# Attention on one core of a Trainium2: features of two heads at a time, and other products ahead of attention's

## The chip, the core and the metric

One core of a Trainium2 chip runs the whole program in one launch. The metric is the time of one execution on the device in microseconds (us); the median of the runs counts. TensorE (PE) multiplies, VectorE (DVE) and ScalarE (ACT) read its results from PSUM (8 banks of 128 partitions x 512 float32), GpSimd (POOL) gathers rows, SyncE (SP) starts transfers.

## The reference

1250 rows of 512 features pass a graph network of three layers, a mixture of 16 experts, a second graph network with linear attention, and a last layer with a choice of 128 of 1024 values. The change is in the third stage, and in a small part of the second:

```python
q, k, v = (heads(h_dense, Wq), heads(h_dense, Wk), heads(h_dense, Wv))   # 256 rows, 8 heads of 64
u = jnp.einsum('bhnd,md->bhnm', t * scale, proj)                         # features, m = 256, for q and for k
kf, qf = jnp.exp(u - diag - max) / np.sqrt(M) + KEPS                     # max: over m for q, over all for k
kv = jnp.einsum('bhnm,bhnd->bhmd', kf, vm)
z = 1.0 / (jnp.einsum('bhnm,bhm->bhn', qf, kf.sum(axis=2)) + KEPS)
attn = jnp.einsum('bhnm,bhmd->bhnd', qf, kv) * z[..., None]
conv_out = jax.nn.relu((A @ xn / deg) @ W_conv + b_conv)                 # A: counts of edges, 1250 x 1250
```

The experts compute `silu(x @ gate) * (x @ up) @ down` for the rows that chose them.

## The kernel before, in words

Every engine has a program written out by hand; semaphores alone tie them together. Rows are kept in 10 tiles of 125. There is no planner: the order of each engine's program is the order of the work, and each engine takes its instructions in that order.

*Preparation of attention* (`tensor`, `vector`). TensorE makes the key features of the 8 heads (`pe_features`, L1987; head h lies on partitions 64 to 127 of its operands where h is odd, on 0 to 63 where it is even) into three banks in turn, VectorE takes their maximum (L1706), and the bank is used again when it has. After heads 2 and 5 a product of z (`pe_conv_z`: one tile of normalised rows times W_conv, L444) is put between. Then the maxima are turned (L2223), z 2 follows, the bias of the keys is spread by a small product (L2226), z 3 follows. Each z is split by ScalarE (`act_z_hi`, L767) and VectorE (`vec_z`, L1103) into a high and a low part.

*The loop over heads.* In turn t (0 to 8) TensorE does `pe_head_products` of head t-1, `pe_head_features` of head t, and `conv_work[t]`: two products of z in turns 0 to 2, one sum over the neighbours in turns 3 to 8 (`pe_conv_sum`, `pe_neighbours`, L1850; 20 products of 125 x 512). `pe_head_products` is: values' product (kf with v, bank 4, L2002), turning of the query features (bank 5, L2010), a wait for ScalarE's copy of them (L879) and VectorE's copy of kv (L1291), attention's product (bank 4 again, L2017). ScalarE takes the exponentials of the features (L866, L872), VectorE scales them (L1276, L1284), finds the query's maximum and bias between (L1278, L1281), and normalises attention's result (L1294 to L1299). ScalarE also copies the edge counts of tile t-2 in turn t (`act_counts`, L778). Banks 0 to 3 hold the features: 0 and 1 for even heads, 2 and 3 for odd ones. After the loop the attention rows are turned (L2244) and the last sums follow.

*The experts' steps* (`pe_step`, 8 executed here). Two experts' rests of 32 rows each are worked on together: gate and up products on strips of 32 columns (L1906), ScalarE's silu (L811), VectorE's product (L1241), turning of the hidden rows (L1915) for each of the two, with the turning of the next rows (L1872) between, VectorE's copies (L1244), down products on strips of 32 columns (L1922). Both hidden parts are turned before the first down product.

## Time and profile before

| | us |
|---|---|
| median of 3 runs | 1354.39 |
| lowest, highest | 1353.56, 1357.17 |
| the profiled execution | 1357.98 |
| its span, first to last instruction | 1356.3 |

| engine | busy us | share of the span |
|---|---|---|
| TensorE, products | 1270.0 | 94% |
| TensorE, loading of weights (beside them) | 835.9 | 62% |
| VectorE | 557.9 | 41% |
| ScalarE | 462.7 | 34% |
| GpSimd | 199.3 | 15% |

The times of the program's span are counted from its first instruction. A product of float32 operands shows as two instructions. A busy TensorE is not TensorE at its peak: it is also busy at half clock, and with few rows or columns. The mean granted clock of the span was 0.98 of 2.4 GHz.

### The profile page before, as it was taken

The numbers are of one execution on the slowest core, as the hardware profiler recorded it, in microseconds if no ns is written. First come the engines' busy times: TensorE is split into PE (matmuls) and PEld (weight loads), VectorE is DVE, ScalarE is ACT, GpSimd is POOL, SyncE is SP. The second block draws the span as 40 slices with busy tenths as digits, with TensorE's granted clock in tenths as the row PEclk, the third lists the DMA queues.
The fourth block names the chain that finished last, engine by engine and source line by source line (L and its number), as shares of the span: only waits on it lengthen the run. The fifth ranks groups of instructions, "written<-read, shape, count | busy, mean of one in ns | idle before, by whom it ended". The sixth has DMA issues, their size and how long they took to land.

```text
span 1356.3 us, 19368 instructions
## 1 busy us (share of the span) xinstructions
PE 1270.0 (94%) x6567; PEld 835.9 (62%) x6568; DVE 557.9 (41%) x1512; ACT 462.7 (34%) x991; POOL 199.3 (15%) x201
## 2 busy tenths in 40 slices
PE   4899999999999999989999999999999999989697
PEld 2454477466556645468877887777465576564465
DVE  8999832211124425100000000001483333686894
ACT  5799643122212210011111111111132232337893
POOL 2000000000000006511111111111543000022480
PEclk8999999999999999999999999999998999999899
DMA  9100000000021120571165213456460000100001
GB/s 220 75 1 1 2 1 1 1 1 1 0 94 31 32 94 2 162 272 58 43 232 200 83 46 137 152 214 221 126 190 19 32 1 1 71 1 0 1 28 50
DMA packets 42949, 98.25 MB, mean 72 GB/s; under 512 B 4113, under 2 KB 6603, under 8 KB 41845
## 3 DMA queue, kind: packets, MB, share of 16 engines
q1 hardware_dynamic: 28613, 68.70, 14.9%
q0 software_dynamic: 6144, 16.45, 4.3%
q10 hardware_dynamic: 8112, 12.08, 2.4%
q8 instruction: 45, 0.74, 0.2%
q14 instruction: 35, 0.29, 0.1%
HBM read 81.02 MB, written 16.17 MB: 72 GB/s over the span
## 4 chain that ended last, share of the span: by engine, by line
PE 72%; DVE 13%; issue 4%; POOL 4%; ACT 3%; DMA 2%; ACTq 1%; DVEq 1%; POOLq 0%
PE psum L444 34%; PE psum L1850 14%; PE psum L1893 7%; PE psum L1830 4%; PE psum L2044 3%; POOL slot_tokens L705 3%; PE psum L1987 2%; DVE sb_hT_conv L1447 1%; PE psum L1922 1%; PE psum L472 1%; ACT sb_htok L828 1%; DVE sb_stats L452 1%; PE psum L1872 1%; POOL sb_blk L649 1%; DVE sb_htok L1336 1%
## 5 line engine op out<-in xcount | busy, mean ns | idle before, releaser
L444 PEld LDWEIGHTS psum<-sb_blk,sb_w_reg 128*128 128x128 f32 x1792 | 204.0, 192 | 14.3 <-issue 14.3
L444 PE MATMUL psum<-sb_blk,sb_w_reg 128*128 128x128 f32 x1792 | 205.2, 275 | 3.2 <-issue 3.2
L1850 PE MATMUL psum<-sb_z_reg_r,sb_hT_conv_r 125*125 125x512 f32 x400 | 169.6, 424 | 0.2 <-issue 0.2
L444 PE MATMUL psum<-sb_w_reg,sb_hT_conv 128*125 128x512 f32 (+1 forms) x376 | 168.9, 599 | 0.0
L1233 DVE TENSOR_TENSOR sb_blk<-sb_blk,psum 128x256 f32<-128x256 f32 x56 | 23.6, 421 | 285.5 <-ACT sb_blk L799 285.5
L1850 PE MATMUL psum<-sb_htok_r,sb_hT_conv_r 125*125 125x512 f32 x300 | 117.8, 393 | 0.0
L444 PEld LDWEIGHTS psum<-sb_w_reg,sb_hT_conv 128*125 128x125 f32 (+1 forms) x376 | 69.0, 189 | 77.5 <-issue 76.9
L444 PE MATMUL psum<-sb_hT_conv,sb_w_reg 128*128 128x416 f32 (+3 forms) x336 | 102.1, 460 | 0.8 <-issue 0.8
L1893 PE MATMUL psum<-sb_w_reg,sb_blk 128*128 128x512 f32 x224 | 100.8, 592 | 0.0
L778 ACT CAST sb_hT_conv_r<-sb_a_reg 125x625 fp32r<-125x625 f32 x80 | 56.1, 715 | 115.0 <-PE psum L1850 115.0
L1850 PEld LDWEIGHTS psum<-sb_z_reg_r,sb_hT_conv_r 125*125 125x125 f32 x400 | 75.1, 188 | 25.1 <-issue 7.7
L2044 PE MATMUL psum<-sb_hT_conv,sb_sil 125*125 125x400 bf16 x316 | 73.1, 356 | 16.0 <-DVE sb_a_reg L1455 7.0
L2044 PEld LDWEIGHTS psum<-sb_hT_conv,sb_sil 125*125 125x125 bf16 x316 | 42.5, 139 | 69.9 <-DVE sb_a_reg L1455 38.3
L444 PEld LDWEIGHTS psum<-sb_hT_conv,sb_w_reg 128*128 128x128 f32 x336 | 63.6, 193 | 34.6 <-issue 31.2
L1830 PE MATMUL psum<-sb_w_reg,sb_hT_conv 128*125 128x512 f32 x160 | 80.4, 593 | 0.8 <-DMA sb_w_reg<-w_gnn 0.8
L1447 DVE TENSOR_SCALAR sb_hT_conv<-sb_sil,sb_blk 125x400 bf16<-125x400 f16 x316 | 81.1, 327 | 0.0
L799 ACT ACTIVATE sb_blk<-psum 128x256 f32<-128x256 f32 x56 | 21.5, 383 | 172.0 <-PE psum L444 172.0
L891 ACT ACTIVATE sb_blk<-sb_sil,sb_blk 125x125 bf16<-125x125 f16 x237 | 77.3, 391 | 7.1 <-DVE sb_blk L1409 5.6
L691 POOL IOTA sb_blk<- 125x160 f32 x1 | 0.3, 307 | 462.2 <-DVE sb_blk L1130 462.2
L1850 PEld LDWEIGHTS psum<-sb_htok_r,sb_hT_conv_r 125*125 125x125 f32 x300 | 55.7, 186 | 17.2 <-issue 4.8
L1893 PEld LDWEIGHTS psum<-sb_w_reg,sb_blk 128*128 128x128 f32 x224 | 40.4, 190 | 40.2 <-issue 40.2
L767 ACT CAST sb_z_reg_r<-psum 125x512 fp32r<-125x512 f32 x40 | 23.3, 583 | 91.8 <-PE psum L444 86.0
(396 smaller groups left out, 1774.8 us busy)
## 6 DMA issues: line engine op xcount, KB each, us to landing
sb_hT_conv<-w_expert SPq DMA_DIRECT2D x7, 2048.0 KB, 8.9
sb_w_reg<-w_expert SPq DMA_DIRECT2D x6, 2048.0 KB, 17.6
sb_hT_conv<-w_expert SPq DMA_DIRECT2D x7, 1024.0 KB
slot_outs<-sb_blk ACTq DMA_DIRECT2D x28, 256.0 KB
sb_w_reg<-w_expert SPq DMA_DIRECT2D x6, 1024.0 KB, 19.4
sb_w_reg<-w_gnn SPq DMA_DIRECT2D x1, 4096.0 KB, 42.6
sb_w_reg<-w_qkv SPq DMA_DIRECT2D x1, 3072.0 KB, 21.6
slot_outs<-sb_blk ACTq DMA_DIRECT2D x1, 2560.0 KB, 10.8
```

Source lines behind the costliest of these rows:

```text
L444: ins = e.matmul(out, l, r, start=(n == 0), stop=(n == len(pairs) - 1))
L705: e.indirect_dma_start(list_dram, bass.IndirectOffsetOnAxis(ap=list_i[:, i, k:k + 1], axis=0), tok_id[:, i:i + 1], None).then_inc(list_sca ...
L767: e.copy(z_hi_rows[i], psum[0:TP, b, :]).then_inc(z_hi, 1)
L778: e.copy(counts_at(l, n), adj[:, h * HALF_T:(h + 1) * HALF_T, tile(i)]).then_inc(counts_in, 1)
L891: e.activation(sq_lo[t % 2][:, j, :], neg_iota, ACT.Square, bias=neg_lo[:, c:c + 1], scale=-1.0).then_inc(lo_squared, 1)
L1233: e.tensor_tensor(hidT[:, 2 * h:2 * h + 2, :].rearrange("p k n -> p (k n)"), silg[:, h, :], psum[:, 1 + h, HF:2 * HF], ALU.mult).then_inc( ...
L1447: e.tensor_scalar(hot_key[n][:, j, :], key_iota, key[:, c:c + 1], None, ALU.is_equal).then_inc(hot_ready, 1)
L1830: ins = e.matmul(psum[0:TP, bank, :], hT[:, k, tile(i)], w_gnn[:, 0 if own else 1, k, :], start=(k == 0), stop=(k == KD - 1))
L1850: ins = e.matmul(psum[0:TP, b, :], counts_at(l, 2 * i + n // NT)[:, s % HALF_T, :], z[s], start=(n == 0), stop=(n == len(pairs) - 1))
L1893: ins = e.matmul(psum[:, 5, :], hidT[:, k, :], w_dn[:, k, :], start=(k == 0), stop=(k == KD - 1))
L1987: ins = e.matmul(psum[:, b, s * 256:(s + 1) * 256], qk[n][rows, h // 2, s * 128:(s + 1) * 128], projT[rows, :], start=True, stop=True)
L2044: ins = e.matmul(psum[0:TP, t % 3, 0:KEYS], hot_lo[n][:, j, :], hot_key[n][:, j, :], start=(j == 0), stop=(j == RUN - 1))
```

## The change

Five things, all in the order and the grouping of instructions; what is computed stays the same.

- Features are made for a pair of heads: the even head's and the odd head's products alternate (rows 0 to 63, rows 64 to 127), each into its own bank, keys first, then queries. In the loop this is done in every second turn. Their semaphore is `features_mm`.
- In the preparation the four pairs follow each other over banks 1 to 4; the products of z come after them, and the small products use banks 5 and 4.
- `pe_head_products` becomes `pe_head_values` (values' product, turning) and `pe_head_attention`. Between the two stand, in even turns, the next pair's features, and in odd turns the first piece of the turn's other work: one z, or half a sum. `pe_neighbours` can be issued in halves.
- VectorE copies kv, then does the next head's features (maximum and bias before the scaling of the keys), then attention's part. Values' product of head h waits for attention's part of head h-1.
- In `pe_step` the second hidden part is turned behind the first down product. The second load of the shared down weights counts on the first one's semaphore.

```diff
@@ -407,9 +407,15 @@
         XN_COEF = KD + 1
         DIAG_MM, KM_MM, KMAX_TURNED, K_BIAS_MM = 1, 9, 10, 11
         MEAN_W, HALF, V_ONES, DIAG, KM_READ, K_MAX8, K_DIAG, K_BIAS = 1, 4, 5, 6, 14, 15, 17, 19
-        head_pe, head_vec, head_act = (sem("head_" + n) for n in ("pe", "vec", "act"))
-        K_MM, Q_MM, KV_MM, QF_TURNED, ATT_MM, PER_HEAD_PE = 1, 2, 3, 4, 5, 5
-        KF, Q_BIAS, QF, KV_IN, ATT, PER_HEAD_VEC = 1, 2, 3, 4, 6, 6
+        head_pe, head_vec, head_act, features_mm = (sem("head_" + n) for n in ("pe", "vec", "act", "features"))
+        KV_MM, QF_TURNED, ATT_MM, PER_HEAD_PE = 1, 2, 3, 3
+        K_MM, Q_MM, PER_PAIR_PE = 2, 4, 4
+        PER_HEAD_VEC = 6
+
+        def vec_at(first, later):
+            return lambda h: first if h == 0 else PER_HEAD_VEC * h + later
+        Q_BIAS_AT, KF_AT, QF_AT = vec_at(1, -1), vec_at(2, 0), vec_at(3, 1)
+        KV_IN_AT, ATT_AT = vec_at(4, 4), vec_at(9, 9)
         KF_EXP, QF_EXP, QFT_IN, PER_HEAD_ACT = 2, 4, 5, 5
         at_turned, attnT_in, ha_mm, ha_in, shifted = (
             sem(n) for n in ("at_turned", "attnT_in", "ha_mm", "ha_in", "shifted"))
...
@@ -1272,23 +1278,25 @@
 
         def vec_head_features(e, h):
             r, bq = h % 2, 2 * (h % 2) + 1
+            e.wait_ge(features_mm, PER_PAIR_PE * (h // 2) + Q_MM)
+            e.tensor_reduce(q_max[:, :, h], psum[:, bq, :].rearrange("p (t m) -> p t m", t=2), AX.X,
+                            ALU.max).then_inc(v_own, v.up())
+            e.wait_ge(v_own, v.n)
+            e.scalar_tensor_tensor(q_bias[:, :, h], diag[:, 0, :, h], -1.0, q_max[:, :, h], ALU.mult,
+                                   ALU.subtract).then_inc(head_vec, 1)
             e.wait_ge(head_act, PER_HEAD_ACT * h + KF_EXP)
             e.tensor_scalar(kf[:, r], kf[:, r], inv_root_m, K_EPS, ALU.mult, ALU.add).then_inc(head_vec, 1)
-            e.wait_ge(head_pe, PER_HEAD_PE * h + Q_MM)
-            e.tensor_reduce(q_max[:, :, h], psum[:, bq, :].rearrange("p (t m) -> p t m", t=2), AX.X,
-                            ALU.max).then_inc(v_own, v.up())
-            e.wait_ge(v_own, v.n)
-            e.scalar_tensor_tensor(q_bias[:, :, h], diag[:, 0, :, h], -1.0, q_max[:, :, h], ALU.mult,
-                                   ALU.subtract).then_inc(head_vec, 1)
             e.wait_ge(head_act, PER_HEAD_ACT * h + QF_EXP)
             e.tensor_scalar(qf[:, r], qf[:, r], inv_root_m, K_EPS, ALU.mult, ALU.add).then_inc(head_vec, 1)
 
-        def vec_head_products(e, h):
+        def vec_head_values(e, h):
             r = h % 2
             e.wait_ge(head_pe, PER_HEAD_PE * h + KV_MM)
             if h >= 2:
                 e.wait_ge(head_pe, PER_HEAD_PE * (h - 2) + ATT_MM)
             e.tensor_copy(kv[:, r].rearrange("p m d -> p (m d)"), psum[:, 4, 0:130]).then_inc(head_vec, 1)
+
+        def vec_head_attention(e, h):
             out = psum[:, 4, 0:130].rearrange("p (t d) -> p t d", t=2)
             e.wait_ge(head_pe, PER_HEAD_PE * h + ATT_MM)
...
@@ -1702,28 +1710,30 @@
                 e.tensor_scalar(hT[:, k, :], hT[:, k, :], bsc[:, k:k + 1], bsh[:, k:k + 1], ALU.mult,
                                 ALU.add).then_inc(xn_ready, 1)
             for h in range(HEADS):
-                e.wait_ge(prep_pe, DIAG_MM + h + 1)
-                e.reduce_max(k_max[:, h:h + 1], psum[:, 1 + h % 3, :], AX.X).then_inc(prep_vec, 1)
-                if h % 3 == 2:
-                    vec_z(e, 3, h // 3, 6 + h // 3 % 2, conv_lo_rows)
+                e.wait_ge(prep_pe, DIAG_MM + h // 2 * 2 + 2)
+                e.reduce_max(k_max[:, h:h + 1], psum[:, 1 + h % 4, :], AX.X).then_inc(prep_vec, 1)
+            vec_z(e, 3, 0, 6, conv_lo_rows)
             e.wait_ge(prep_pe, KMAX_TURNED)
-            e.reduce_max(k_max8, psum[0:HEADS, 4, 0:128], AX.X).then_inc(prep_vec, 1)
+            e.reduce_max(k_max8, psum[0:HEADS, 5, 0:128], AX.X).then_inc(prep_vec, 1)
             e.wait_ge(prep_vec, K_MAX8)
             e.tensor_scalar(k_diag, ident[0:HEADS, 0:HEADS], k_max8, None, ALU.mult).then_inc(prep_vec, 1)
             e.memset(ones8, 1.0).then_inc(prep_vec, 1)
-            vec_z(e, 3, 2, 6, conv_lo_rows)
+            vec_z(e, 3, 1, 7, conv_lo_rows)
             e.wait_ge(prep_pe, K_BIAS_MM)
             for s in range(2):
-                e.scalar_tensor_tensor(k_bias[:, s, :], diag[:, 1, s, :], -1.0, psum[:, 5, 0:HEADS], ALU.mult,
+                e.scalar_tensor_tensor(k_bias[:, s, :], diag[:, 1, s, :], -1.0, psum[:, 4, 0:HEADS], ALU.mult,
                                        ALU.subtract).then_inc(prep_vec, 1)
-            vec_z(e, 3, 3, 7, conv_lo_rows)
+            for i in range(2, Z_BEFORE):
+                vec_z(e, 3, i, 6 + i % 2, conv_lo_rows)
             e.wait_ge(ld_norms, 3 * 16)
 
             for t in range(HEADS + 1):
                 for h in of_tiles(t, 1, 0, HEADS):
-                    vec_head_products(e, h)
+                    vec_head_values(e, h)
                 for h in of_tiles(t, 0, 0, HEADS):
                     vec_head_features(e, h)
+                for h in of_tiles(t, 1, 0, HEADS):
+                    vec_head_attention(e, h)
                 for what, i in conv_work[t]:
                     if what == "z":
...
@@ -1832,26 +1842,31 @@
             if k == KD - 1:
                 ins.then_inc(self_mm if own else z_mm, 1)
 
-        def pe_neighbours(e, flag, l, i, b, lo_rows):
+        def pe_neighbours(e, flag, l, i, b, lo_rows, halves=(0, 1)):
 
             pairs = [(s, z) for s in range(NT) for z in (z_hi_rows, lo_rows)]
+            steps = range(halves[0] * NT, (halves[-1] + 1) * NT)
             with e.If(flag > 0):
-                for n, (s, z) in enumerate(pairs):
+                for n in steps:
+                    s, z = pairs[n]
                     if n % NT == 0:
                         e.wait_ge(counts_in, 2 * (l * NT + i) + n // NT + 1)
                     ins = e.matmul(psum[0:TP, b, :], adj[:, s, tile(i)], z[s].bitcast(F32), start=(n == 0), stop=(n == len(pairs) - 1))
...
@@ -1910,12 +1925,11 @@
             e.wait_ge(ld_down[LAST_SLOT], landing)
             e.wait_ge(s_y, g + 1)
             e.wait_ge(s_he, g * 2 + 2)
-            for n in range(2):
+            for n, (_, w_dn) in enumerate((b, a_)):
                 e.wait_ge(s_hid, g * 2 + n + 3)
                 e.transpose(psum[:, 3 + n, 0:128], hid[:, n * 128:(n + 1) * 128], ident).then_inc(s_ht, 1)
                 if n == 0:
                     pe_turn_rows(e, g + 1)
-            for n, (_, w_dn) in enumerate((b, a_)):
                 e.wait_ge(s_he, g * 2 + n + 3)
                 for k in range(KD):
                     for c in range(PER_BLOCK):
...
@@ -1949,11 +1963,17 @@
                 e.wait_ge(z_lo, 3 * NT + i - 1)
             pe_z(e, 3, i, w_conv, 6 + i % 2)
 
-        def pe_conv_sum(e, flag, i):
+        def pe_conv_sum(e, flag, i, halves=(0, 1)):
             e.wait_ge(z_lo, 4 * NT)
             if i >= 2:
                 e.wait_ge(conv_added, i - 1)
-            pe_neighbours(e, flag, 3, i, 6 + i % 2, conv_lo_rows)
+            pe_neighbours(e, flag, 3, i, 6 + i % 2, conv_lo_rows, halves)
+
+        def pe_conv_work(e, flag, what, i, half):
+            if what == "z":
+                pe_conv_z(e, i)
+            else:
+                pe_conv_sum(e, flag, i, (half,))
 
         def pe_busy(e, b, operand, n, rows=128):
...
@@ -1981,28 +2001,31 @@
             if c % 2 == 1 or c == IN_PAIRS - 1:
                 ins.then_inc(ia_mm, 1)
 
-        def pe_features(e, n, h, b):
-            rows = slice(64 * (h % 2), 64 * (h % 2) + 64)
+        def pe_features(e, n, p, banks, done):
+
             for s in range(2):
-                ins = e.matmul(psum[:, b, s * 256:(s + 1) * 256], qk[n][rows, h // 2, s * 128:(s + 1) * 128],
-                               projT[rows, :], start=True, stop=True)
-            return ins
-
-        def pe_head_features(e, h):
-            if h >= 2:
-                e.wait_ge(head_act, PER_HEAD_ACT * (h - 2) + QF_EXP)
-            pe_features(e, 1, h, 2 * (h % 2)).then_inc(head_pe, 1)
-            pe_features(e, 0, h, 2 * (h % 2) + 1).then_inc(head_pe, 1)
-
-        def pe_head_products(e, h):
+                for odd in range(2):
+                    rows = slice(64 * odd, 64 * odd + 64)
+                    ins = e.matmul(psum[:, banks[odd], s * 256:(s + 1) * 256], qk[n][rows, p, s * 128:(s + 1) * 128],
+                                   projT[rows, :], start=True, stop=True)
+                    if s == 1:
+                        ins.then_inc(done, 1)
+
+        def pe_pair_features(e, p):
+            if p >= 1:
+                e.wait_ge(head_act, PER_HEAD_ACT * (2 * p - 1) + QF_EXP)
+            pe_features(e, 1, p, (0, 2), features_mm)
+            pe_features(e, 0, p, (1, 3), features_mm)
+
+        def pe_head_values(e, h):
             r = h % 2
-            e.wait_ge(head_vec, PER_HEAD_VEC * h + KF)
+            e.wait_ge(head_vec, KF_AT(h) if h == 0 else ATT_AT(h - 1))
             for m in range(2):
                 for s in range(2):
                     ins = e.matmul(psum[:, 4, m * 65:(m + 1) * 65], kf[:, r, s, m * 128:(m + 1) * 128],
                                    v_ext[:, s, h, :], start=(s == 0), stop=(s == 1))
             ins.then_inc(head_pe, 1)
-            e.wait_ge(head_vec, PER_HEAD_VEC * h + QF)
+            e.wait_ge(head_vec, QF_AT(h))
             if h >= 1:
                 e.wait_ge(head_act, PER_HEAD_ACT * (h - 1) + QFT_IN)
...
@@ -2010,8 +2033,11 @@
                     ins = e.transpose(psum[:, 5, m * 256 + s * 128:m * 256 + (s + 1) * 128],
                                       qf[:, r, s, m * 128:(m + 1) * 128], ident)
             ins.then_inc(head_pe, 1)
+
+        def pe_head_attention(e, h):
+            r = h % 2
             e.wait_ge(head_act, PER_HEAD_ACT * h + QFT_IN)
-            e.wait_ge(head_vec, PER_HEAD_VEC * h + KV_IN)
+            e.wait_ge(head_vec, KV_IN_AT(h))
             for s in range(2):
                 for m in range(2):
...
@@ -2213,31 +2239,34 @@
             ins.then_inc(prep_pe, 1)
             e.wait_ge(ld_proj, 4 * 16)
             e.wait_ge(ld_wconv, 16)
-            for h in range(HEADS):
-                if h >= 3:
-                    e.wait_ge(prep_vec, DIAG + h - 2)
-                pe_features(e, 1, h, 1 + h % 3).then_inc(prep_pe, 1)
-                if h % 3 == 2:
-                    pe_conv_z(e, h // 3)
+            for p in range(HEADS // 2):
+                if p >= 2:
+                    e.wait_ge(prep_vec, DIAG + 2 * p - 2)
+                pe_features(e, 1, p, (1 + 2 * (p % 2), 2 + 2 * (p % 2)), prep_pe)
+            pe_conv_z(e, 0)
             e.wait_ge(prep_vec, KM_READ)
-            e.transpose(psum[0:HEADS, 4, 0:128], k_max, ident).then_inc(prep_pe, 1)
-            pe_conv_z(e, 2)
+            e.transpose(psum[0:HEADS, 5, 0:128], k_max, ident).then_inc(prep_pe, 1)
+            pe_conv_z(e, 1)
             e.wait_ge(prep_vec, K_DIAG)
-            e.matmul(psum[:, 5, 0:HEADS], ones8, k_diag, start=True, stop=True).then_inc(prep_pe, 1)
-            pe_conv_z(e, 3)
+            e.matmul(psum[:, 4, 0:HEADS], ones8, k_diag, start=True, stop=True).then_inc(prep_pe, 1)
+            for i in range(2, Z_BEFORE):
+                pe_conv_z(e, i)
 
             e.wait_ge(prep_vec, K_BIAS)
             e.wait_ge(hT_in, 5 * NT)
             for t in range(HEADS + 1):
+                beside = [("z", i, None) if what == "z" else (what, i, half) for what, i in conv_work[t]
+                          for half in ((None,) if what == "z" else (0, 1))]
                 for h in of_tiles(t, 1, 0, HEADS):
-                    pe_head_products(e, h)
-                for h in of_tiles(t, 0, 0, HEADS):
-                    pe_head_features(e, h)
-                for what, i in conv_work[t]:
-                    if what == "z":
-                        pe_conv_z(e, i)
-                    else:
-                        pe_conv_sum(e, flag, i)
+                    pe_head_values(e, h)
+                if t % 2 == 0 and t < HEADS:
+                    pe_pair_features(e, t // 2)
+                else:
+                    pe_conv_work(e, flag, *beside.pop(0))
+                for h in of_tiles(t, 1, 0, HEADS):
+                    pe_head_attention(e, h)
+                for work in beside:
+                    pe_conv_work(e, flag, *work)
             e.wait_ge(head_vec, PER_HEAD_VEC * HEADS)
             for s in range(2):
                 for k in range(KD):
```

Left out: the same halves in the other branch of `pe_neighbours`, ScalarE's waits (for `features_mm` and `Q_BIAS_AT(h)`), and the renamed semaphore.

## Rows read from the trace of the kernel before

**Rows 1.** The page, part 4: shares of the chain that ended last, by engine.

```profile
PE 72%; DVE 13%; issue 4%; POOL 4%; ACT 3%; DMA 2%; ACTq 1%; DVEq 1%; POOLq 0%
```

**Rows 2.** Chain of waits in order of time: start us, us, engine, what, line.

```profile
1045.81 7.06 PE psum L444 x16
...
1078.71 0.60 ACT sb_w_reg L879
...
1080.46 3.71 PE psum L1987 x8
1084.17 6.25 PE psum L1850 x20
1090.42 0.84 PE psum L2002 x8
1091.26 0.46 PE psum L2010 x4
...
1091.74 0.59 ACT sb_w_reg L879
...
1092.38 1.11 PE psum L2017 x8
1093.48 1.92 PE psum L1987 x8
1095.41 4.84 PE psum L1850 x20
...
1139.07 0.88 PE psum L2244 x8
```

**Rows 3.** Stretches: length, busy of each engine, PEclk, DMA share, GB/s.

```profile
1019.00:1025.60 6.60, 6.56 (x17) 3.80 (x17) 4.34 (x10) 2.75 (x2) 2.06 (x2) 0.50 0.19 73
...
1080.60:1087.10 6.50, 6.50 (x15) 4.68 (x16) 2.42 (x8) 2.81 (x6) 0.00 (x0) 0.50 0.07 26
1114.70:1118.00 3.30, 3.30 (x8) 2.15 (x8) 1.71 (x4) 1.90 (x6) 0.00 (x0) 0.51 0.00 0
```

**Rows 4.** Timeline of PE, whole and cut at 0.25 us (first, last two).

```profile
1043.82 0.48 PE L1987 MATMUL psum<-sb_blk,sb_w_reg 64*128 64x256 f32 x1
...
1027.96 0.49 PE L1987 MATMUL psum<-sb_blk,sb_w_reg 64*128 64x256 f32 x2
...
1019.15 3.77 PE L1987 MATMUL psum<-sb_blk,sb_w_reg 64*128 64x256 f32 x12
...
1027.96 1.99 PE L1987 MATMUL psum<-sb_blk,sb_w_reg 64*128 64x256 f32 x12
...
1036.18 0.27 PE L2223 MATMUL psum<-sb_ident,sb_blk 128*8 128x128 f32 x1 [1.53 <-DVE sb_blk L1706]
```

**Rows 5.** Timeline of DVE, preparation and one turn of the loop.

```profile
1020.17 1.77 DVE L1702 TENSOR_SCALAR sb_hT_conv<-sb_hT_conv,sb_blk 128x1250 f32<-128x1250 f32 x2
1021.86 1.88 DVE L1706 TENSOR_REDUCE sb_blk<-psum 128x1 f32<-128x512 f32 x3
...
1093.92 0.47 DVE L1299 TENSOR_SCALAR sb_blk<-psum,sb_blk 128x64 f32<-128x64 f32 x2
...
1097.58 0.43 DVE L1284 TENSOR_SCALAR sb_w_reg<-sb_w_reg 128x512 f32<-128x512 f32 x1 [0.91 <-ACT sb_w_reg L872]
```

**Rows 6.** Timeline of all engines: one of the experts' steps.

```profile
683.70 0.33 PE L1915 MATMUL psum<-sb_ident,sb_blk 128*128 128x128 f32 x1
...
683.86 0.60 PE L1872 MATMUL psum<-sb_ident,sb_blk 128*128 128x128 f32 x4
684.07 0.29 DVE L1244 COPY sb_blk<-psum 128x128 f32<-128x128 f32 x1 [0.42 <-PE psum L1915]
...
684.61 0.33 PE L1915 MATMUL psum<-sb_ident,sb_blk 128*128 128x128 f32 x1
...
684.86 1.08 PE L1922 MATMUL psum<-sb_hT_conv,sb_blk 128*32 128x128 f32 x32
...
687.00 0.44 PE L1922 MATMUL psum<-sb_w_reg,sb_blk 128*32 128x128 f32 x5 [0.20 <-issue]
```

More of the change, by code:

```diff
@@ L354, in build @@
         ld_edges, ld_x, ld_w0, ld_w1, ld_router = (sem("ld_" + n) for n in ("edges", "x", "w0", "w1", "router"))
-        ld_shared_up, ld_shared_down, ld_kept = (sem("ld_shared_" + n) for n in ("up", "down", "down_again"))
+        ld_shared_up, ld_shared_down = (sem("ld_shared_" + n) for n in ("up", "down"))
         ld_up = [sem(f"ld_slot{n}_up") for n in range(3)]
@@ L860, in act_head_features @@
             r, bk, bq = h % 2, 2 * (h % 2), 2 * (h % 2) + 1
-            e.wait_ge(head_pe, PER_HEAD_PE * h + K_MM)
+            e.wait_ge(features_mm, PER_PAIR_PE * (h // 2) + K_MM)
             e.wait_ge(prep_vec, K_BIAS)
@@ L867, in act_head_features @@
                              bias=k_bias[:, s, h:h + 1]).then_inc(head_act, 1)
-            e.wait_ge(head_vec, PER_HEAD_VEC * h + Q_BIAS)
+            e.wait_ge(head_vec, Q_BIAS_AT(h))
             if h >= 2:
@@ L964, in scalar @@
             e.wait_ge(x_shared, SHARED_NOW)
-            e.dma_start(w_kept, a["w_shared"][:, W_UP:].rearrange("p (k n) -> p k n", k=KD)).then_inc(ld_kept, 16)
+            e.dma_start(w_kept, a["w_shared"][:, W_UP:].rearrange("p (k n) -> p k n", k=KD)).then_inc(ld_shared_down, 16)
             turns, end = turns_of(e)
@@ L1274, in vec_head_features @@
             r, bq = h % 2, 2 * (h % 2) + 1
-            e.wait_ge(head_act, PER_HEAD_ACT * h + KF_EXP)
-            e.tensor_scalar(kf[:, r], kf[:, r], inv_root_m, K_EPS, ALU.mult, ALU.add).then_inc(head_vec, 1)
-            e.wait_ge(head_pe, PER_HEAD_PE * h + Q_MM)
+            e.wait_ge(features_mm, PER_PAIR_PE * (h // 2) + Q_MM)
             e.tensor_reduce(q_max[:, :, h], psum[:, bq, :].rearrange("p (t m) -> p t m", t=2), AX.X,
@@ L1282, in vec_head_features @@
                                    ALU.subtract).then_inc(head_vec, 1)
+            e.wait_ge(head_act, PER_HEAD_ACT * h + KF_EXP)
+            e.tensor_scalar(kf[:, r], kf[:, r], inv_root_m, K_EPS, ALU.mult, ALU.add).then_inc(head_vec, 1)
             e.wait_ge(head_act, PER_HEAD_ACT * h + QF_EXP)
             e.tensor_scalar(qf[:, r], qf[:, r], inv_root_m, K_EPS, ALU.mult, ALU.add).then_inc(head_vec, 1)
-        def vec_head_products(e, h):
+        def vec_head_values(e, h):
             r = h % 2
@@ L1844, in pe_neighbours @@
                         ins.then_inc(half_mm, 1)
-                ins.then_inc(neigh_mm, 1)
+                if 1 in halves:
+                    ins.then_inc(neigh_mm, 1)
             with e.Else():
-                for n, (s, z) in enumerate(pairs):
+                for n in steps:
+                    s, z = pairs[n]
                     if n % NT == 0:
@@ L1853, in pe_neighbours @@
                         ins.then_inc(half_mm, 1)
-                ins.then_inc(neigh_mm, 1)
+                if 1 in halves:
+                    ins.then_inc(neigh_mm, 1)
         def pe_shared_up(e, n):
@@ L2169, in tensor @@
             e.matmul(psum[0:1, 7, 0:2], ident[:, 0:1], ident[:, 0:2], start=True, stop=True).then_inc(experts_over, 1)
-            e.wait_ge(ld_kept, 16)
+            e.wait_ge(ld_shared_down, 32)
             for i in range(SHARED_NOW, NT - 1):
```

## The prediction

> **What bounds the kernel now.** The chain that ended last is read first: TensorE has 72% of it and VectorE 13% [rows 1]. Then the chain in order of time, through the stretch that the change rewrites, from the first head's features (1043.89, which is 1045.81 - 1.92) to the turning of the attention rows (1139.07): 95.18 us, all on TensorE but for one short piece of ScalarE per head [rows 2]. One turn of that loop reads: values' product 0.84 (L2002), turning of the query features 0.46 (L2010), a wait of 0.66 for ScalarE's copy (1091.72 to 1092.38, L879), attention's product 1.11 (L2017), the next head's features 1.92 (L1987), one neighbour sum 4.84 (L1850): 9.83 us. VectorE and ScalarE are never late there except for that copy. So what counts is how much TensorE has to do in this loop, what it waits for, and at what clock it does it; the granted clock is the third view [rows 3].
>
> **The change, part by part.** The profiled execution took 1357.98 us (span 1356.3), 3.6 above the median of 1354.39 and 0.8 above the slowest of the timed runs; savings are worked out against the profiled one.
>
> *Features of two heads at once, in the loop.* A head's features are 8 instructions on 64 rows, each after the other: 1.92. Do instructions on the other 64 rows run beside them? The trace of before shows it by accident. In the preparation three heads' key features stand in a row (rows 64 to 127, 0 to 63, 64 to 127), and in the first 0.2 us of that group two instructions have begun and take 0.49 together, while in the loop one alone takes 0.48 in the same time [rows 4]. Also the next such group's 12 instructions take 1.99, where 8 of the loop take 1.92 [rows 2, 4]: 4 pairs and then 4 alone, 8 places of 0.24. With the new order 16 instructions of a pair of heads fill 8 places: 1.92 for two heads. 8 x 1.92 becomes 4 x 1.92: **7.7 us** less. Bounds: 0 (no overlap when they alternate) to 7.7.
>
> *Other work ahead of attention's product.* The wait of 0.66 after each turning is now covered by the pair's features (1.92) or half a sum (4.84 / 2 = 2.4) or a product of z (7.06 / 2 = 3.5) [rows 2]; the copy ends 0.66 behind the turning in each case. 8 x 0.66 = 5.3. In turn 3 the copy begins only at 1078.71, behind two copies of counts on ScalarE, 0.4 later than usual: this goes too. **5.7 us**. What could be late next: values' product of head h now waits for VectorE to have normalised head h-1, because attention's result and values' product share a bank. In the shorter, odd turns attention's product ends 1.30 + 2.4 + 1.11 = 4.8 into the turn; VectorE needs about 1.1 more (5.9; today its normalising ends 1094.39, 0.9 behind the product's end) [rows 2, 5], and TensorE comes back at 4.8 + 2.4 = 7.2. Cover 1.3 us. The exponentials: a pair's query features are ready 3.2 into an even turn, then reduction, bias, two exponentials and scaling end some 2.7 later, at 5.9 (today 1098.01 against 1095.40, the features' end) [rows 2, 5], and the turn lasts 9.2; the second head of the pair has all of the next turn. VectorE's new order (maximum of the queries before scaling the keys, attention's part last) costs TensorE nothing while these covers stand. The halves of the sums take six more branches and changes of shape; I put 0.3 us on them, 0 to 2.
>
> *The preparation.* Before: groups of 12, 12 and 8 instructions, 20 places; now 16 in one row. The first 8 places run at half clock (3.77, or 0.47 each) [rows 3, 4]. Pairs 0 and 1 end at 1019.2 + 8 x 0.47 = 1023.0, but pair 2 needs VectorE to have read heads 0 and 1, and VectorE is busy with the scaling (L1702) until 1021.9; its reductions come every 0.6 from 1021.86 on [rows 5], so pair 2 starts at about 1023.15, a new idle time of 0.2, and pair 3 ends at about 1026.6. The four products of z (7.06 / 2 [rows 2] and a little, 3.6 each) and 0.6 for the two small products end at 1041.6, against 1043.89: 2.3 less. The idle 1.53 for VectorE's reductions at 1036.18 [rows 4] is inside that: the last two reductions now lie under the first z. Against it: the low clock ended at 1025.6 when z had been running; if it now lasts 3 us more into z, 1.6 of the 2.3 is lost. I take **1.5 us**, from -0.5 to 3.
>
> *The experts' inner turning.* There are 8 such steps. Now the second turning waits for the second hidden part (0.91 after the first) and the down products of both halves start only behind it, at 1.16 [rows 6]. With the new order the first down product needs the four turnings of rows (0.76) and VectorE's copy (0.37 + 0.29): 0.76 instead of 1.16. Its 32 instructions take 0.9 (1.08 with the last one's tail), then the second turning (0.33), VectorE's copy (0.29) and three hand-overs of 0.04 are bare: the second down product starts at 2.4 and has 0.9 to go, 3.3; today all is issued 3.74 after the first turning, 0.4 of it a gap without a wait inside the second product ("issue") [rows 6]. If the gap stays, 3.7, if it falls under the wait, 3.3. So 0 to 0.4 less per step, 3.2 for eight at best. The Trainium skill, TensorEngine Tiling (Array Packing), Key Properties, speaks against this part: changing the tiling mode drains TensorE, and the second turning (full array) now stands between two products on strips of 32 columns. The trace agrees in kind: from the second turning to the first strip product it is 0.25, where the row turnings follow each other every 0.11 [rows 6]. Two more changes per step at 0.15 to 0.25 are 0.3 to 0.5, and eight steps lose 0 to 4 in place of winning. Between both I take **0.5 us** less, from -4 to +3.
>
> *The clock.* In the loop it falls to half twice, for 6.5 and 3.3 us [rows 3]. The first costs 3.71 - 1.92 + 6.25 - 4.84 = 3.2 [rows 2], the second about half its length, 1.6. Both came soon after TensorE stood waiting for ScalarE's copy. The account closes: 4 x 1.92 + 3 x 7.06 + 6 x 4.84 + 8 x 1.30 + 8 x 1.11 = 77.2 is the loop after, without waits or low clock; 95.2 - 77.2 = 18.0, and 7.7 + 5.7 + 4.8 = 18.2. Without the waits I expect fewer dips, but not surely none; half of 4.8 is **2.4 us**, bounds -5 to 4.8. The faster of the timed runs may have had fewer already, which is one more reason for half.
>
> *The rest.* One semaphore for the shared weights in place of two changes no order. Behind the loop the chain goes on on TensorE with the turning of the attention rows [rows 2], so what is saved ahead of it arrives at the end.
>
> **Sum.** 7.7 + 5.7 - 0.3 + 1.5 + 0.5 = 15.1 in work and waits, 2.4 in clock: 17.5. From the median 1354.39: 1336.9, told as 1337.
>
> **Rivals.**
> - *Heads don't overlap when they alternate.* Each even turn costs 3.84 for features: 7.7 less gain, 1344.6. Against it: the two-at-once start in [rows 4]. Chance 0.06.
> - *A new wait takes the place of the old.* TensorE, faster by a sixth, waits in each turn for VectorE's normalising (bank 4) or for a sum's counts. Cover is 1.3 us, and ScalarE and VectorE have some 4 us of work in a turn of 7.2. With 0.5 per turn: 4 us back, 1341. Chance 0.10.
> - *The steps get slower*, by the drain above and the bare turning: 0.5 each, 4 us in place of 0.5 gained: 1341.4. Chance 0.10.
> - *The clock wins.* No dip in the loop and an early end of the low stretch in the preparation: 2.4 + 0.8 more: 1333.7. Chance 0.16.
> - *The other side: the clock loses.* Two row halves at work and a denser loop could bring the lower level more often; work at it takes twice the time. The loop's 77 us would have to run 36 us or more of it at half clock to eat 18 us; the dips now are 9.8 us in 95. At 40 us, 20 us lost: 1357. Against it: the dips followed waits, and the dense stretch of z in the loop ran at full clock. Chance 0.03.
> - *My forecast*, all parts nearly as worked out: 0.55.
>
> **How the numbers follow.** A measurement of this kernel tells about 0.3% (4 us) from no change. Every case but the clock's loss and part of the unforeseen is below 1350.3. Faster 0.94, within 0.3% 0.03, slower 0.03. The range reaches from the clock's gain with a good preparation and steps (1330) to the missing overlap (1345).
>
> **What would show it.** In the chain, L1987 as x16 pieces of about 1.9 us, four of them; no ScalarE piece (L879's line) between turning and attention's product; even turns of about 9.2 and odd ones of about 7.2 us; 77 to 80 us from the first pair to the attention rows' turning; the preparation 1.5 to 2.3 shorter; the second turning of a step about 1.7 behind the first, and all issued 3.3 to 3.8 behind it. Pairs of 3.8 us, idle time before values' product released by VectorE, or steps over 4.2 us would show the forecast wrong, as would more than 10 us at clock 0.5 in the loop.

## The result, and the profile after

| | before | after |
|---|---|---|
| median (range, runs) | 1355.78 (1353.56 to 1361.57, 4) | 1332.76 (1331.69 to 1333.83, 4) |
| ratio, 95% interval | | 0.9842 (0.9807 to 0.9877) |
| profiled execution, span | 1357.98, 1356.3 | 1333.69, 1331.9 |

23.0 us less; 17.4 were forecast. The whole interval of the ratio lies below 1. Cut at the same instructions of TensorE, the two profiled spans compare like this (us):

| stretch | before | after | |
|---|---|---|---|
| up to the first expert step | 582.91 | 585.68 | +2.8 |
| experts, to the last step's first turning | 370.83 | 366.74 | -4.1 |
| from there to the 32 small products | 61.77 | 60.41 | -1.4 |
| the small products | 3.64 | 3.55 | -0.1 |
| preparation: first key features to the loop | 24.67 | 22.17 | -2.5 |
| loop: first pair to the attention rows' turning | 95.09 | 74.92 | -20.2 |
| the rest | 217.39 | 218.43 | +1.0 |

The first and last lines are stretches that the change doesn't touch: they differ by 1 to 4 us from one execution to the next (the kernel before, traced again below, had 586.66 and 219.3 there). The third line varies from 58.9 to 62.6 over all traces; here the mean granted clock was 0.94 before and 1.00 after, and the change has no part in it but the last step's 0.4 more.

The chain of waits after, from the end of turn 2 on (start us, us, engine, what, line; L2009 features, L1864 sums, L2025 values' product, L2033 turning, L2043 attention's product):

```profile
1060.89 6.93 PE psum L450 x16
...
1068.46 0.70 DVE sb_z_last L1109
...
1069.48 2.59 PE psum L1864 x10
1072.07 0.84 PE psum L2043 x8
1072.91 2.38 PE psum L1864 x10
1075.30 0.84 PE psum L2025 x8
1076.14 0.44 PE psum L2033 x4
1076.58 1.93 PE psum L2009 x16
1078.51 1.04 PE psum L2043 x8
1079.54 4.70 PE psum L1864 x20
1084.24 0.84 PE psum L2025 x8
1085.08 0.44 PE psum L2033 x4
1085.52 2.31 PE psum L1864 x10
1087.84 0.84 PE psum L2043 x8
1088.68 2.38 PE psum L1864 x10
...
1113.64 0.87 PE psum L2273 x8
```

Against [rows 2]: features come as x16 in 1.93, what x8 took; ScalarE's copy is gone from between turning and attention's product. An even turn is 1075.30 to 1084.24, 8.9 us; an odd one 6.8 (9.2 and 7.2 forecast). Attention's product takes 0.84 behind half a sum and 1.04 behind a pair's features, where it took 1.11 behind the wait. One short wait is left, for the last z's low part in turn 3 (VectorE's 0.70); TensorE is idle for 0.4 us in the whole loop.

The granted clock (columns as in [rows 3]), in the preparation and in the whole loop:

```profile
1017.00:1023.90 6.90, 6.11 (x30) 4.11 (x26) 5.78 (x10) 2.75 (x2) 2.41 (x2) 0.51 0.19 74
1038.60:1113.50 74.90, 74.51 (x394) 54.70 (x394) 32.71 (x89) 31.91 (x63) 0.00 (x0) 1.00 0.04 15
```

The loop is at 2.4 GHz throughout, the two stretches at 1.2 GHz of before are gone; the one in the preparation is still there. It is not that after's execution had less of the low clock as a whole: the mean of the span is 0.979, before's was 0.980. Ahead of the first expert step it was 0.97 after and 0.99 before. TensorE in the preparation (timeline; against [rows 4] 1019.15 and 1036.18):

```profile
1016.38 3.24 PE L2009 MATMUL psum<-sb_blk,sb_w_reg 64*128 64x256 f32 x16
1020.42 3.65 PE L2009 MATMUL psum<-sb_blk,sb_w_reg 64*128 64x256 f32 x16 [0.80 <-DVE sb_blk L1714]
```

The third pair waits 0.80 for VectorE's reductions (0.2 forecast); the old idle 1.53 is gone. What holds VectorE up is the small products' result (timeline of VectorE):

```profile
1016.49 0.19 DVE L1698 COPY sb_blk<-psum 128x32 f32<-128x32 f32 x1 [1.28 <-PE psum L2237]
...
1017.40 1.77 DVE L1710 TENSOR_SCALAR sb_hT_conv<-sb_hT_conv,sb_blk 128x1250 f32<-128x1250 f32 x2
1019.09 2.48 DVE L1714 TENSOR_REDUCE sb_blk<-psum 128x1 f32<-128x512 f32 x4
```

One of the experts' steps after (timeline; against [rows 6]):

```profile
685.86 0.33 PE L1930 MATMUL psum<-sb_ident,sb_blk 128*128 128x128 f32 x1
686.02 0.60 PE L1887 MATMUL psum<-sb_ident,sb_blk 128*128 128x128 f32 x4
...
686.57 1.08 PE L1936 MATMUL psum<-sb_hT_conv,sb_blk 128*32 128x128 f32 x32
...
687.58 0.33 PE L1930 MATMUL psum<-sb_ident,sb_blk 128*128 128x128 f32 x1
687.95 0.29 DVE L1250 COPY sb_blk<-psum 128x128 f32<-128x128 f32 x1 [1.24 <-PE psum L1930]
...
688.29 1.08 PE L1936 MATMUL psum<-sb_w_reg,sb_blk 128*32 128x128 f32 x32 [0.38 <-DVE sb_blk L1250]
689.19 0.19 PE L1952 MATMUL psum<-sb_ident 128*1 128x2 f32 x2
```

The first down product starts 0.71 behind the turning (before 1.16), the second at 2.43, and the step is over at 3.33. In the profiled execution of before it was over at 3.68, with the gap inside. ("Over" is where the next product, the one with 2 columns, starts.) Read alone, the two profiles say that the move of the turning won 4.1 us. The experiments say something else.

### The profile page after: what moved, and what is told of

The parts are those of the page before. It is cut to its first block, busy times and chain, and to the rows that moved or that the text cites. A ratio compares the mean times of both kernels' runs of the same rounds, so it can differ in the third digit from the quotient of the medians.

```text
span 1331.9 us, 19378 instructions
## 1 busy us (share of the span) xinstructions
PE 1255.2 (94%) x6567; PEld 828.1 (62%) x6568; DVE 557.6 (42%) x1512; ACT 462.4 (35%) x991; POOL 198.8 (15%) x201
## 4 chain that ended last, share of the span: by engine, by line
PE 73%; DVE 13%; POOL 4%; issue 4%; ACT 2%; DMA 2%; ACTq 1%; DVEq 1%; POOLq 0%
PE psum L450 34%; PE psum L1864 14%; PE psum L1908 7%; PE psum L1840 4%; PE psum L2070 4%; POOL slot_tokens L711 3%; PE psum L478 1%; PE psum L1936 1%; PE psum L1887 1%; DVE sb_hT_conv L1455 1%; ACT sb_htok L834 1%; DVE sb_stats L458 1%; DVE sb_x_res L1269 1%; PE psum L1981 1%; POOL sb_blk L655 1%
## 5 line engine op out<-in xcount | busy, mean ns | idle before, releaser
L1864 PE MATMUL psum<-sb_z_reg_r,sb_hT_conv_r 125*125 125x512 f32 x400 | 169.0, 423 | 0.6 <-DVE sb_z_last L1109 0.4
L1864 PE MATMUL psum<-sb_htok_r,sb_hT_conv_r 125*125 125x512 f32 x300 | 118.8, 396 | 0.0
L1864 PEld LDWEIGHTS psum<-sb_z_reg_r,sb_hT_conv_r 125*125 125x125 f32 x400 | 74.7, 187 | 23.0 <-issue 5.4
L1864 PEld LDWEIGHTS psum<-sb_htok_r,sb_hT_conv_r 125*125 125x125 f32 x300 | 56.3, 188 | 17.3 <-issue 4.8
```

Of the source, the lines that this page charges most:

```text
L1864: ins = e.matmul(psum[0:TP, b, :], counts_at(l, 2 * i + n // NT)[:, s % HALF_T, :], z[s], start=(n == 0), stop=(n == len(pairs) - 1))
```

## The experiments

Each kernel was traced once and, where a range is given, timed in several runs beside the kernel before on the same chip. Ratios are to that one.

### The old order of the steps inside the new kernel

```diff
-            for n, (_, w_dn) in enumerate((b, a_)):
+            for n in range(2):
                 e.wait_ge(s_hid, g * 2 + n + 3)
                 e.transpose(...).then_inc(s_ht, 1)
                 if n == 0:
                     pe_turn_rows(e, g + 1)
+            for n, (_, w_dn) in enumerate((b, a_)):
                 e.wait_ge(s_he, g * 2 + n + 3)
```

> The kernel after, with the experts' inner turning put back as before. In the trace of after the stretch from the first gate product of the steps to the last step's first turning is 366.7 us, before it was 370.8; the last step went from 2.94 to 3.33 us. If the moved turning did that, the stretch is 370.8 again and the time is 3.7 above after's 1332.8 (1336.5). If the 4.1 us are noise of the stretch (transfers, gathers), it stays near 366.7 to 367.5 and the time within 1 us of after's.

Measured: 1330.46 (1329.15 to 1331.20), ratio 0.9836 (0.9794 to 0.9878). The steps' stretch was 363.87 us, 2.9 less than after and 7 less than before, and in the last step the last down product began 2.84 behind the first turning where after it was 3.24. Both expectations missed: in the trace the old order is the faster one, and the 370.8 of before must have had something else in it. The times cannot tell the two orders apart here (0.9836 against 0.9842, with intervals of 0.0035 and more to each side).

### The moved turning alone, and the kernel before once more

The first is the kernel before with the diff above the other way round; the second is the kernel before unchanged; the third has only the one semaphore for both loads of the shared down weights.

> The kernel before with only the experts' inner turning moved. The old order run inside the new kernel took 363.9 us from the first gate product of the steps to the last step's first turning, where the new kernel took 366.7 and the kernel before 370.8: old and new order cannot both be the cause. Theory A, the new order itself costs (two more changes of tiling mode, bare turning): at equal supply of instructions 2.9 us more; here 366.7 if the kernel's gap without a wait (0.46 in the down product, 0.7 behind it) is gone with any change of placement, 370 to 374 if it stays. Theory B, the new order saves 4.1 us by itself: 366.7 and the rest as before. They part by the gap: under A a gap over 0.3 without a wait may stand in the down product beside the bare turning of 0.71. Time within 4 us of before.

> The kernel before, once more, for its trace. If the gap of 0.46 in the down product of each step (and 0.7 behind it) belongs to the program's placement, it is there again and the stretch of the steps is 370.8; if it is of the moment (other transfers), the stretch lies anywhere from 363.9 to 370.8. Same for the two stretches at half clock in the loop: fixed at the same turns, or wandering.

> The kernel before with the one semaphore for both loads of the shared down weights, and nothing else. Up to the experts' end TensorE's instructions are then those of the new kernel with the old steps (363.9 us) but for what comes behind. If the semaphore's numbering does it, the stretch is 363.9; if the code behind the loop does it, 370.8 as before.

| | steps' stretch | loop | time |
|---|---|---|---|
| before, profiled execution | 370.83 | 95.09 | 1357.98 |
| before, again | 363.27 | 95.05 | 1354.79 |
| one semaphore | 364.00 | 92.02 | 1351.68 |
| moved turning alone | 366.67 | 99.88 | 1360.74 (1352.83 to 1364.82), ratio 1.0019 (0.9992 to 1.0046) |

The very same kernel took 7.6 us less in the steps' stretch the second time. The stretch holds seven whole steps. Its timeline of TensorE in one of them, against [rows 6]:

```profile
685.80 0.33 PE L1915 MATMUL psum<-sb_ident,sb_blk 128*128 128x128 f32 x1
685.97 0.60 PE L1872 MATMUL psum<-sb_ident,sb_blk 128*128 128x128 f32 x4
686.71 0.33 PE L1915 MATMUL psum<-sb_ident,sb_blk 128*128 128x128 f32 x1
686.97 1.08 PE L1922 MATMUL psum<-sb_hT_conv,sb_blk 128*32 128x128 f32 x32
687.87 1.06 PE L1922 MATMUL psum<-sb_w_reg,sb_blk 128*32 128x128 f32 x32
688.74 0.19 PE L1938 MATMUL psum<-sb_ident 128*1 128x2 f32 x2
```

64 down instructions without a break, and the step is over at 2.94, not 3.68. The gap "issue" of [rows 6] belonged to that one execution (and with it about 0.3 more behind each step), not to the order nor to the program; the eighth step of that same execution took 2.94 too. What made the gap stays open. The moved turning costs 3.33 against 2.94 in each step (in the sixth, longer in every trace, 3.6 against 3.2 to 3.3): 366.7 in all eight traces with it, 363.3 to 364.0 in five of the six with the old order. That is the rival "the steps get slower", at 0.4 per step. The forecast's own sum for the new order, 3.3, has no drain in it and meets the 3.33. The rule of the Trainium skill weighed there (TensorEngine Tiling (Array Packing), Key Properties: a change of tiling mode drains TensorE) points the same way; no run here parts the drain from the bare turning and copy. The time of the moved turning alone can't show it: its median is 3.2 above that of before, as seven or eight steps of 0.4 would make it, but the interval of the ratio holds 1 as well, and the low clock in the loop (99.88 in place of 95.1) moves by more than that from one execution to the next.

### Pairs without the other work ahead, and the other work ahead without pairs

In the first, `pe_head_attention` stands straight behind `pe_head_values`; pairs, preparation and steps as after. In the second, every turn has one head's features between the two, keys and then queries, as before (both edits are shown shortened).

```diff
                 for h in of_tiles(t, 1, 0, HEADS):
                     pe_head_values(e, h)
+                    pe_head_attention(e, h)          # first kernel
-                if t % 2 == 0 and t < HEADS:
-                    pe_pair_features(e, t // 2)
+                if t < HEADS:                        # second kernel
+                    pe_head_features(e, t)
```

> The kernel after, with attention's product straight behind the turning again (pairs kept). The loop took 75.0 us after, 95.2 before. Both theories have the wait of 0.66 back eight times, and turn 3's 0.4: loop 80.5 to 81. Theory A, the two stretches at half clock in the loop came from TensorE's waits: they come back and the loop takes 83 to 86. Theory B, they came from features on one half of the rows: none, loop 80.5 to 81. Time 1338.5 (B) to 1343 (A).

> The kernel after, with each head's features made alone, one head per turn as before (deferral kept, the preparation as after). Features take 8 x 1.92 in place of 4 x 1.92: loop 82.7 without a stretch at half clock (theory A, waits cause them), 85 to 88 with one or two (theory B, features on half of the rows cause them). Time 1340.5 (A) to 1345 (B). If two heads did not overlap in the kernel after, the loop would stay at 75.

Measured: without the deferral 1343.17 (1337.57 to 1347.99), ratio 0.9922 (0.9897 to 0.9947), loop 82.07; single heads 1342.38 (1340.84 to 1345.70), ratio 0.9918 (0.9893 to 0.9943), loop 82.77. The loops' stretches:

```profile
1036.40:1118.47 82.07, 76.23 (x393) 55.05 (x393) 32.42 (x89) 31.88 (x63) 0.00 (x0) 1.00 0.04 14
```

```profile
1038.92:1121.69 82.77, 82.77 (x393) 60.31 (x393) 32.41 (x89) 32.67 (x63) 0.00 (x0) 1.00 0.04 14
```

Theory A is that TensorE's waits bring the stretches at half clock, theory B that features on half of the rows bring them. Both profiled executions had the full clock in the loop: theory A wanted low stretches in the first, theory B in the second, and neither was there. Without the deferral TensorE is idle for 5.8 of 82 us; with single heads for none. By these loops the pairs are worth 82.77 - 74.92 = 7.9 and the deferral 82.07 - 74.92 = 7.2. And the waits do show in the turn (chain of waits of the kernel without the deferral):

```profile
1094.12 0.46 PE psum L2033 x4
...
1094.60 0.59 ACT sb_w_reg L885
...
1095.23 1.11 PE psum L2043 x8
```

By the medians the two kernels are 10.4 and 9.6 above after, more than the loops account for; the rest was not traced. The ten timed runs of each say a little more on the clock. Without the deferral four took 1337.6 to 1339.2 with a mean clock of 0.983 to 0.987 and six took 1342.8 to 1348.0 with 0.973 to 0.978; the profiled one was of the first kind. With single heads eight of ten lie within 2.9 us, all ten within 4.9. The kernel after has all four within 2.1. The spread of 10.4 without the deferral would fit theory A, but it decides nothing: over the ten runs the mean clock is 0.980 in both kernels, the low clock in a timed run can lie outside the loop, and kernels whose waits are covered spread by up to 7.5 too (the last of those below).

### The waits of the kernel before filled with work

```diff
             ins.then_inc(head_pe, 1)
+            pe_busy(e, 2 * r, a_reg[0:TP, 0:512], 1, TP)
             e.wait_ge(head_act, PER_HEAD_ACT * h + QFT_IN)
```

> The kernel before, with one product of no use (125 x 512, 0.86 us) put behind each turning of the query features, so that TensorE works in place of waiting 0.66 for ScalarE's copy. The 8 fillers cost about 0.3 us each over the wait, 2.4 in all. Theory A, the waits bring the stretches at half clock: the loop has none, takes 92 to 93 us (95.1 - 4.9 + 2.4), and the times of this kernel lie close together (within 4 us) where those of before spread over 14; its clock is 0.98 or more in every run. Theory B, single heads' features on 64 rows bring them: 97 us and more, with the spread of before. Time against before's on the same chip: 2 us less (A) to 3 more (B).

Measured: 1351.04 (1347.94 to 1358.28), ratio 0.9974 (0.9949 to 0.9998); loop 90.40. The chain of waits in one turn:

```profile
1090.23 0.84 PE psum L2002 x8
1091.07 0.44 PE psum L2010 x4
1091.51 0.86 PE psum L1961 x2
1092.37 0.92 PE psum L2018 x8
1093.29 1.92 PE psum L1987 x8
1095.21 4.87 PE psum L1850 x20
```

The filler (0.86) and attention's product right behind it (0.92) take together what the wait and the product behind it took (0.66 + 1.11): it costs nothing, where 2.4 us were expected. The loop's mean clock:

```profile
1036.00:1127.00 91.00, 90.75 (x410) 62.95 (x409) 33.08 (x89) 32.70 (x63) 0.00 (x0) 1.00 0.04 13
```

The four traces with single heads and bare waits all had stretches at 1.2 GHz in the loop: 9.8 us in before, the same number of stretches in before again (loop clock 0.95 in both), fewer with one semaphore (0.98), most with the moved turning alone (0.90). None of the nine traces with the waits covered or filled had one, and in two of the nine, this one and the one of single heads, features were made one head at a time; the one trace with pairs and bare waits had none either. So low stretches were seen only where single heads and bare waits stood together. Features on half of the rows do not bring them by themselves, which is against theory B. More work in the loop did not make the kernel slower and probably made it faster (the interval ends just below 1): theory A's sign. Its size was only half seen: nine of ten runs lie within 4.9 us, one 10 above the lowest, and the clock was 0.973 to 0.983, not 0.98 and up, since stretches outside the loop stay.

### Head by head within a pair

```diff
-            for s in range(2):
-                for odd in range(2):
+            for odd in range(2):
+                for s in range(2):
```

> The kernel after, where a pair's products are issued head by head (4 instructions of the even head, then 4 of the odd one) and not alternating. If TensorE takes up the other row half's work ahead by itself, as the preparation of the kernel before showed, the 16 instructions still take 1.93 and the time is after's within 1 us. If alternating is needed, a pair takes up to 3.84: loop 75 to 82.7, time up to 7.7 more.

Measured: 1335.92 (1332.59 to 1338.19), ratio 0.9878 (0.9832 to 0.9923); loop 75.33. In the first 0.2 us of a pair two instructions have begun (timeline of TensorE, cut), where one head's instructions alone have only one in that time ([rows 4]). So the second must be the odd head's first, four places further on in the program. The pair takes 2.03 in place of 1.93 (chain of waits):

```profile
1038.92 0.49 PE L2009 MATMUL psum<-sb_blk,sb_w_reg 64*128 64x256 f32 x2
```

```profile
1038.99 2.03 PE psum L2009 x16
```

Over a distance of four instructions TensorE took up the other row half's work by itself; alternating is worth 0.1 per pair, 0.4 in the loop.

### The old preparation

The preparation's part of the diff undone in both engines.

> The kernel after with the preparation of attention as before (three banks, z between). From the first features to the loop it took 24.7 us before and 22.2 after: 24.7 again, the loop 75.0, time 2.5 above after's 1332.8. If the preparation's gain came from where the clock fell, it shows in the granted clock: low from the first features on for 6.6 us in both.

Measured: 1335.64 (1333.83 to 1337.36), ratio 0.9856 (0.9818 to 0.9893); preparation 24.66, loop 74.92. The 2.5 us are the preparation's own. The low stretch begins with the first features, as it did before. The other traces agree: five kernels with this new preparation took 22.2 to 22.5, the six with the old one 24.7 to 25.5. The new one hardly feels where the low clock falls, for it waits for VectorE: in four of those five the first two pairs took 2.0 to 2.1 in place of 3.24, at full clock, and then the third pair waited 1.9 to 2.0 in place of 0.80.

### Further on in the preparation

First VectorE's copy of the small products' result is put behind the scaling of the rows; then also two pairs ahead of the small products; then also the old order of the steps.

```diff
-            e.wait_ge(prep_pe, DIAG_MM)
-            e.tensor_copy(diag..., psum[:, 0, 0:4 * HEADS]).then_inc(prep_vec, 1)
...
                 e.tensor_scalar(hT[:, k, :], hT[:, k, :], bsc[:, k:k + 1], bsh[:, k:k + 1], ...)
+            e.wait_ge(prep_pe, DIAG_MM)
+            e.tensor_copy(diag..., psum[:, 0, 0:4 * HEADS]).then_inc(prep_vec, 1)
```

> The kernel after, with VectorE's copy of the 32 small products' result put behind the scaling of the rows, which it does not need. After: VectorE stood until the small products' end (1016.49), scaled until 1019.2, and the third pair of heads waited for its reductions until 1020.4. Now the scaling can begin some 2 us earlier; the third pair's wait of about 0.8 goes, and first features to loop takes 21.3 in place of 22.2. If the half clock there lasts longer for it (less idle, same low activity), 22. Time 0 to 1 us less than after's.

> As the one before, and the first two pairs' key features ahead of the 32 small products (2 columns each), behind which TensorE's clock was half in every trace so far (6.6 to 7.5 us). At full clock two pairs take 1.9 in place of 3.4 to 3.6. From the small products' or the pairs' start to the loop it took 25.7 us after (3.55 + 22.17): 23 to 24 here. If the clock falls as much with the small products in the middle, the two later pairs stay at 3.6 and z 0 may be hit: 24.5 to 25. Time 1 to 2.7 us below after's ratio to before (0.9842).

> As the one before, with the experts' inner turning put back as it was. Traces so far: the steps' stretch is 366.7 with the moved turning in all six traces, and 363.3 to 364.0 with the old order in three, 370.8 in a fourth (the profiled execution of before), where a gap without a wait stood in each step; the last step is 0.4 shorter. Theory A, the move costs by itself: 3.2 us less than the kernel before this one, in traces (363.5) and times. Theory B, the gap hits the old order often enough in unprofiled runs that both come out even.

| | small products or first pairs to loop | time | ratio |
|---|---|---|---|
| after | 25.7 | 1332.76 | 0.9842 (0.9807 to 0.9877) |
| copy later | 24.0 | 1333.93 (1333.86 to 1335.62) | 0.9845 (0.9810 to 0.9880) |
| pairs first | 25.4 | 1336.71 (1332.75 to 1339.59) | 0.9861 (0.9832 to 0.9890) |
| pairs first, old steps | 26.7 | 1331.15 (1327.83 to 1335.33) | 0.9816 (0.9786 to 0.9847) |

The later copy gave 1.8 us in its place, twice what was expected. Not all of it need be the copy's: the low stretch there lasted 3.4 us in this trace and 6.8 in after's. In the time it gave nothing: in its trace the rest took 221.4 in place of 218.4, with a stretch at 1.2 GHz of 7 us at 1146 that after's trace does not have. Pairs first won 1.2 on the first pairs (2.00 in place of 3.24) and lost it on the next wait (timeline of TensorE):

```profile
1014.12 2.00 PE L2009 MATMUL psum<-sb_blk,sb_w_reg 64*128 64x256 f32 x16
1016.05 3.73 PE L2240 MATMUL psum<-sb_blk,sb_w_reg 128*128 128x2 f32 x32
1021.35 3.64 PE L2009 MATMUL psum<-sb_blk,sb_w_reg 64*128 64x256 f32 x16 [1.57 <-DVE sb_blk L1714]
```

The third pair waits 1.57 for VectorE, whose reductions now stand behind the small products' copy, and the clock is half there as ever, from 1021.3 to 1024.7. The 6.6 to 7.5 us of the expectation are too narrow for the traces: the low stretch behind the small products lasted from 3.4 to 10.2 us in them. The last kernel has the old steps: its stretch is 363.90 against 366.72, and it is 5.6 us faster in the median than the one beside it (2.8 + 0.4 expected from the traces; their intervals still overlap a little). It has the lowest ratio of all, but its interval overlaps that of after: a faster version than the kernel after is likely, not shown.

## Why the prediction was right, point by point

The time, 1332.76, lies in the range and 4.2 below the forecast. The mechanism was right in the loop and in the preparation, which is where the gain is; it was wrong in the steps, and that the sum came out near is in part luck, since the loss there was made up by more clock and more deferral than forecast. By its steps:

- *Pairs*, 7.7: right. 7.9 by the kernel with single heads; x16 in 1.93.
- *Other work ahead*, 5.7 less 0.3: 7.2. The waits went as forecast. What was missed is that attention's product behind other work takes 0.84 to 1.04 and not 1.11, eight times (1.3 or so), and that the branches of the half sums cost nothing (two halves take 4.70, a whole one took 4.84).
- *VectorE's cover* held: no piece in the loop's chain waits for its normalising.
- *Preparation*, 1.5: 2.5. The low clock did not last longer (6.8 us in both traces), and the four pairs filled it. The wait for VectorE's reductions was 0.8, not 0.2, since the scaling could begin only when the small products were through, later against the pairs than assumed.
- *Steps*, 0.5 won: the one step that failed. It costs 0.4 in each of eight, 3.2 us. The forecast took the gap in the down product for the step's own and let the new order hide it; it was a feature of the one execution that was profiled, and there of seven steps in eight. Against an old step without the gap (2.94) the sum of this very part, 3.3, gives the loss rightly.
- *Clock*, 2.4: the loop lost both low stretches, 95.09 - 90.40 = 4.7 by the kernel with filled waits. Their account (4.8) was right, the halving of it too careful: this is the first half of the rival "the clock wins"; its second half, an early end of the low stretch in the preparation, did not come. What took the stretches away is less sure than that they went: with single heads, covering the waits was enough in two traces, and whether pairs alone would have been is not settled. The 49 runs of the kernel before beside the experiments have clocks from 0.969 to 0.985 and times from 1347.9 to 1364.1; a straight line through them gives 8.2 us for each 0.01 of mean clock. Their mean clock is 0.976 and that of the kernel after's four runs 0.981, which by that line would be some 4 us: an estimate, and near the 4.7 of the loop.

The errors lean to one side except the steps: +0.2 in the pairs, +1.8 in the deferral, +1.0 in the preparation, +2.3 in the clock and -3.7 in the steps make +1.6. The gain was 5.6 above the forecast; the other 4 are within the interval of the ratio (0.0035 is 4.7 us): 1.4 of them is the median of before, raised by its fourth run (1361.57) behind the forecast, the rest was not traced. Not settled: whether pairs alone, without covering the waits, already make the stretches at half clock rarer. The one trace of that kernel has none in the loop, but six of its ten runs had a clock of 0.978 or less.

## What to carry to other kernels

Put independent work between a product and the copy that its successor waits for: here it gave back the wait and up to 0.27 in the product behind it, and in the kernel with single heads the stretches at half clock went with the waits. Products on 64 rows cost half when another head's stand on the other 64, alternating or up to four instructions further on. Before a gap without a wait ("issue") goes into a sum, look whether a second trace of the same kernel has it.

## What the runs showed of the hardware

- A gap without a wait in a loop body stood in seven of its eight passes in one execution and in none in another of the same program: 3.68 us in place of 2.94 in the pass shown, 7.6 us over seven passes with what stood behind each.
- In every trace TensorE is at 1.2 GHz for 3 to 10 us in one stretch that begins beside or behind the 32 products of 2 columns and ahead of the first z, also with two pairs of features at full clock straight ahead of them. In before it began as they ended, with single heads in the loop 5.4 us later, with the moved turning alone 2 us before their end.
- Eight products without use, put into waits, did not lengthen the loop (90.40 in place of 95.09 us in the traces), and the kernel became slightly faster if anything: ratio 0.9974 (0.9949 to 0.9998).
- Two products on different halves of the rows, four instructions apart in the program, begin within 0.2 us of each other: 16 of them take 2.03 us, alternating 1.93, and 8 on one half alone 1.92.
